# A gated recurrent step on one core: extra products in two places, half-width sampling pieces, one vector instruction moved up

## The reference, cut to what matters

```
def cell(h, x):
    gi = x @ W_ih + b_ih
    gh = h @ W_hh + b_hh
    i_r, i_z, i_n = jnp.split(gi, 3, axis=-1)
    h_r, h_z, h_n = jnp.split(gh, 3, axis=-1)
    r = jax.nn.sigmoid(i_r + h_r)
    z = jax.nn.sigmoid(i_z + h_z)
    n = jnp.tanh(i_n + r * h_n)
    h_new = (1.0 - z) * n + z * h
    return (h_new, h_new)
...
ix = (grid + 1.0) * 0.5 * (L - 1)
x0 = jnp.floor(ix)
w1 = ix - x0
w0 = 1.0 - w1
...
return w0[:, None, :] * v0 + w1[:, None, :] * v1
```

## Time and profile before

| | us |
|---|---|
| median of 3 runs | 2564.22 |
| the profiled execution's own time | 2577.34 |
| span of the profile (first to last instruction) | 2575.6 |
| the loop of 512 steps (first and last r sum A) | 956.6 to 2552.6 |
| PE busy over the span | 2264.0 (88%) |
| DVE, ACT, POOL busy | 1877.2, 1276.6, 526.3 |

### The profile page before, as it was taken

How to read it: one execution, slowest core, us unless ns; L and a number is a source line. 1 busy time by engine, 2 the same in 40 slices (tenths; PEclk the granted TensorE clock), 3 DMA queues, 4 the chain that set the end, 5 groups by cost and what they waited for, 6 DMA issues and landing times. The chain is left out here.

```text
span 2575.6 us, 139739 instructions
## 1 busy us (share of the span) xinstructions
PE 2264.0 (88%) x58516; PEld 1928.8 (75%) x58516; DVE 1877.2 (73%) x8659; ACT 1276.6 (50%) x5568; POOL 526.3 (20%) x2217
## 2 busy tenths in 40 slices
PE   2563689789797889999899999999999999999998
PEld 2552355454454469889899999999999999999996
DVE  5997684683855957887778777777777767777776
ACT  3542484583754744444444544444444444444443
POOL 1002100100101423333322222222222222222221
PEclk9998799899898999999999999999999999999999
DMA  6000000000001000000000000000000000000000
GB/s 230 2 3 1 0 1 1 0 2 1 1 1 49 1 18 5 5 5 5 5 5 5 9 5 9 9 5 9 9 5 9 5 9 9 5 9 9 5 13 20
DMA packets 17205, 32.08 MB, mean 12 GB/s; under 512 B 9664, under 2 KB 9664, under 8 KB 16320
## 3 DMA queue, kind: packets, MB, share of 16 engines
q1 hardware_dynamic: 14320, 22.08, 2.4%
q10 hardware_dynamic: 2256, 1.06, 0.2%
HBM read 18.94 MB, written 4.19 MB: 9 GB/s over the span
## 5 line engine op out<-in xcount | busy, mean ns | idle before, releaser
L1720 PE MATMUL psum<-parts1A,region_w_hh 128*128 128x40 f16 x12288 | 433.1, 179 | 18.7 <-DVE parts1A L1390 12.0
L1720 PE MATMUL psum<-parts0A,region_w_hh 128*128 128x40 f16 x12288 | 434.1, 179 | 16.7 <-DVE parts0A L1390 10.0
L1720 PE MATMUL psum<-parts0B,region_w_hh 128*128 128x40 f16 x12288 | 435.8, 179 | 8.6 <-issue 2.9
L1720 PE MATMUL psum<-parts1B,region_w_hh 128*128 128x40 f16 x12288 | 434.1, 179 | 7.8 <-DVE parts1B L1390 1.9
L1720 PEld LDWEIGHTS psum<-parts1A,region_w_hh 128*128 128x128 f16 x12288 | 373.3, 96 | 29.8 <-DVE parts1A L1390 18.6
L1720 PEld LDWEIGHTS psum<-parts0A,region_w_hh 128*128 128x128 f16 x12288 | 373.2, 96 | 25.7 <-DVE parts0A L1390 14.8
L792 ACT ACTIVATE mixA<-rzA 128x8 f32<-128x8 f32 x512 | 111.0, 217 | 565.5 <-DVE rzA L1342 565.5
L1720 PEld LDWEIGHTS psum<-parts0B,region_w_hh 128*128 128x128 f16 x12288 | 364.4, 96 | 28.6 <-issue 7.5
L1720 PEld LDWEIGHTS psum<-parts1B,region_w_hh 128*128 128x128 f16 x12288 | 362.9, 96 | 26.0 <-DVE parts1B L1390 10.5
L1342 DVE TENSOR_REDUCE rzA<-psum 128x8 f32<-128x32 f32 x512 | 97.6, 191 | 189.3 <-PE psum L1720 179.6
L485 POOL TENSOR_TENSOR addA<-zA,lineA 128x8 f32<-128x8 f32 x512 | 104.5, 204 | 592.5 <-ACT zA L799 592.5
(11 more groups left out here) (257 smaller groups left out, 4047.3 us busy)
## 6 DMA issues: line engine op xcount, KB each, us to landing
region_rows<-in_x_dram SPq DMA_DIRECT2D x4, 1024.0 KB, 12.4
out_dram<-region_w_b SPq DMA_DIRECT2D x16, 256.0 KB, 2.0
region_w_a<-in_L_cond_W_qkv_dram SPq DMA_DIRECT2D x1, 3072.0 KB, 20.0
region_rows<-in_L_cond_W_ih_dram SPq DMA_DIRECT2D x1, 3072.0 KB, 10.8
region_cols<-in_L_cond_W_emb_dram SPq DMA_DIRECT2D x1, 2048.0 KB, 12.8
region_scratch<-in_L_cond_W_hh_dram SPq DMA_DIRECT2D x2, 768.0 KB, 6.2
region_cond<-in_cond_dram ACTq DMA_DIRECT2D x1, 1024.0 KB, 6.4
region_w_out<-in_L_cond_W_out_dram SPq DMA_DIRECT2D x1, 1024.0 KB, 22.1
```

The lines of the kernel that those rows point to most:

```text
L1720: made = e.matmul(k.slots(bank)[:, :, ch, :, 0:2], k.w16[:, part, 2 * read + c, 6 * half + 2 * "rzn".index(g) + ch], k.parts[now][read][:, ...
```

## The change

Three things change, all in the recurrent loop.

1. The extra products stand in two places of a step, after unit ABr and after unit BBn (`SIDE_AFTER`), one contraction chunk in each, where before both chunks stood behind BBn. The same products are made, in the same two steps.
2. The sampling jobs are 160 pieces over 128 steps: each DVE instruction covers 256 columns instead of 512, and five pieces stand in four steps, one in each of three steps and two in the fourth (step 3, 7, 11, ...). Each piece waits for the one before it (`grid`). POOL's two additions keep their 512 and 128 columns; they are queued in the step in which DVE makes the last half of `part`, and wait for it.
3. On DVE keep A stands ahead of r B.

The diff, cut to its core:

```diff
-def sampling_job(j):
-
-    b, r = divmod(j, 24)
-    return (b, r, None) if r < 12 else (b, 12 + (r - 12) % 3, (r - 12) // 3)
+def sampling_job(i):
+
+    j, half = divmod(i, 2)
+    b, r = divmod(j, 20)
+    return (b, r, None, half) if r < 12 else (b, 12 + r % 2, (r - 12) // 2, half)
+
+SAMPLING_JOBS = 160
+
+def sampling_jobs(st):
+
+    return range(min(5 * st // 4, SAMPLING_JOBS), min(5 * (st + 1) // 4, SAMPLING_JOBS))
...
         pool_state(e, k, st, 1)
-        if st < 96:
-            b, r, c = sampling_job(st)
-            if r == 14:
+        for i in sampling_jobs(st):
+            b, r, c, part = sampling_job(i)
+            if r == 13 and part == 1:
                 to = k.sampling[:, b, c]
                 n = 2 * (NC * b + c)
-                e.wait_ge(s["grid"], grid_count(b, 13, c))
+                e.wait_ge(s["grid"], i + 1)
...
-    if r == 14:
-        return
-    if job == 0:
+    cols = slice(half * D // 2, (half + 1) * D // 2)
+    place, fl, integer, left, nxt = (t[:, b, cols] for t in (k.place, k.whole, k.as_int, k.w0, k.right))
+    if i == 0:
         e.wait_ge(s["grid_in"], 16)
     else:
-        e.wait_ge(s["grid"], n - 1)
+        e.wait_ge(s["grid"], i)
...
         dve_n_line(e, k, st, 0)
+        dve_keep(e, k, st, 0)
         dve_r_sum(e, k, st, 1)
-        dve_keep(e, k, st, 0)
         dve_high(e, k, st, 0, nxt)
...
-        if st < 96:
-            dve_sampling_job(e, k, st)
+        for i in sampling_jobs(st):
+            dve_sampling_job(e, k, i)
...
+SIDE_AFTER = ("ABr", "BBn")
...
-        if st in SIDE:
-            (kind, *args), part, parity = SIDE[st]
-            number += part == 0
-            ks = (0, 1) if part == 0 else (2, 3)
...
+            if st in SIDE and u in SIDE_AFTER:
+                (kind, *args), part, parity = SIDE[st]
+                c = 2 * part + SIDE_AFTER.index(u)
+                number += c == 0
```

More of the change, by code:

```diff
@@ L91, in bases_before @@
     return sum(has_base(m) for m in range(n))
-def grid_count(b, r, k):
-    return 20 * b + (r + 1 if r < 12 else 12 + 2 * k + r - 11)
 def side_groups(q):
@@ L1213, in dve_split_inputs, with dve_sampling_job @@
     e.scalar_tensor_tensor(low, source, k.xs[2][:], high, ALU.mult, ALU.subtract).then_inc(s["x_low"], 1)
-def dve_sampling_job(e, k, job):
+def dve_sampling_job(e, k, i):
     s = k.sem
-    b, r, c = sampling_job(job)
-    n = grid_count(b, r, c)
-    place, fl, integer, left, nxt = k.place[:, b], k.whole[:, b], k.as_int[:, b], k.w0[:, b], k.right[:, b]
-    if r == 14:
-        return
-    if job == 0:
+    b, r, c, half = sampling_job(i)
+    cols = slice(half * D // 2, (half + 1) * D // 2)
+    place, fl, integer, left, nxt = (t[:, b, cols] for t in (k.place, k.whole, k.as_int, k.w0, k.right))
+    if i == 0:
         e.wait_ge(s["grid_in"], 16)
     else:
-        e.wait_ge(s["grid"], n - 1)
+        e.wait_ge(s["grid"], i)
     if r == 0:
@@ L1252, in dve_sampling_job @@
         e.wait_ge(s["gates_in_sum"], 12)
-        e.scalar_tensor_tensor(k.sampling[:, b, c], fl, k.feature[:, c:c + 1], left, ALU.is_equal, ALU.mult).then_inc(s["grid"], 1)
+        e.scalar_tensor_tensor(k.sampling[:, b, c, cols], fl, k.feature[:, c:c + 1], left, ALU.is_equal, ALU.mult).then_inc(s["grid"], 1)
     else:
@@ L1257, in dve_sampling_job @@
             e.wait_ge(s["sampling"], 2 * before + 1)
-        e.scalar_tensor_tensor(k.part[:, c % 2], nxt, k.feature[:, c:c + 1], place, ALU.is_equal, ALU.mult).then_inc(s["grid"], 1)
+        e.scalar_tensor_tensor(k.part[:, c % 2, cols], nxt, k.feature[:, c:c + 1], place, ALU.is_equal, ALU.mult).then_inc(s["grid"], 1)
 def dve_add_states(e, k, tile, b, c):
@@ L1724, in pe_gru @@
                 made.then_inc(s[f"{g}_products{h}"], 1)
-        if st in SIDE:
-            (kind, *args), part, parity = SIDE[st]
-            number += part == 0
-            ks = (0, 1) if part == 0 else (2, 3)
[L1729 to L1732, removed]
+            if st in SIDE and u in SIDE_AFTER:
+                (kind, *args), part, parity = SIDE[st]
+                c = 2 * part + SIDE_AFTER.index(u)
+                number += c == 0
+                if kind == "gates":
+                    pe_gate_group(e, k, *args, (c,), SIDE_BANK[parity], number)
+                else:
+                    pe_rows_group(e, k, *args, (c,), SIDE_BANK[parity], number)
 def build(nc, *args):
```

## The result

The changed kernel takes 2597.11 us, the median of 4 runs (2594.74 to 2598.38). The kernel before, run beside it, takes 2562.88 (4 runs, 2561.09 to 2564.81). The ratio is 1.0132, with an interval of 1.0115 to 1.0150: **34.2 us slower**. The forecast was 24.8 us slower, with a range of 2570 to 2604.

The account below looks back on a forecast made before the run. A chain of small instructions through all engines, not PE, was taken to set the step. The terms 2 + 8.7 + 6 + 10.3 + 0.8 - 3 gave +24.8 us on the median 2564.2, so 2589.0 us, range 2570 to 2604.

Parts of the forecast that it names:

- What bounds the kernel: A loop of small instructions through all engines sets the step, 3.01 us; half of the extra products are off it.
- faster by PE: Rival for the whole loop: PE sets the step, so moving extra products gains 43 us, 2529 in all; chance 0.10.
- (a): Extra products in two places, 16-bit steps: a tie, 3.015 instead of 3.01 us, +2 us over 360 steps.
- (b): Extra products in two places, 32-bit steps: half of them takes 0.30 us, +0.09 a step over 96 steps, +8.7 us.
- (c): Gaps among PE's A products, no longer absorbed by the wait for low B: +6 us, bounds 0 and 9.
- (d): POOL's additions start later, waiting for the same step's half piece, and delay its multiplication for A: +10.3 us.
- (e): DVE's half pieces ahead of r sum A: single halves cost nothing, two in a row do; +0.8 us.
- (f): Keep A ahead of r sum B on DVE: high A no longer delayed where r sum B is late, -3 us.
- The lock: Rival: keep A, starting first, blocks POOL's multiplication; high A 0.2 us later in 512 steps, 2690; chance 0.02.
- the argument from keep B: Keep B starts 0.05 us before POOL's multiplication, which runs inside its 0.27 us, so keep A would not block POOL.

Follow-up runs that it names:

- the second profile of before: The kernel before, unchanged, run again for another profile: 2560.29 against 2560.62 us, ratio 1.0001; its profiled execution took 2559.6.
- the shift: Kernel before plus 20 one-column memsets at the start of DVE's program: 2560.57 us, ratio 0.9990; with keep A first as well: 2568.52, ratio 1.0032.
- the spread halves: Kernel before, POOL's additions spread over three steps, DVE's wide pieces halved, never two a step: 2548.57 us; with keep A first as well: 2557.84.
- its two variants: Changed kernel with POOL's additions queued one step later: 2589.38 us, ratio 1.0103; with them spread over three steps: 2579.38 us, ratio 1.0074.
- the first profile of before: The kernel before, unchanged, as profiled for the prediction: that execution took 2577.34 us, against a median of 2564.2.

## Why the prediction was right in sign and short in size

**What bounds the kernel** held. Half of the extra work was off the path, the A start went back to 1.99 as in the earlier trace rows, and the rival "faster by PE" is out: the two places alone cost 8.8 us. POOL's 0.4 behind the B start and high A's 0.33 behind its multiplication came as written.

**(a) and (b), extra products.** Forecast 2 and 8.7. Against the steps without extra products of the same profile (3.013) the changed kernel's steps give 360 x 0.006 = 2.2 and 96 x 0.087 = 8.4; against the second profile of before (3.007) they give 4.3 and 8.9. The choice of 0.30 for half of the 32-bit products was right: the row shows 0.31.

**(c), gaps laid bare.** This is the term that was wrong in sign for the edit alone. The count failed first: I took 86 gaps from one profile as a property of the kernel. A second profile of the same kernel has 44, the kernel with two places 15 and the changed one 37. With 8.8 measured and 11.2 to 11.8 from the steps, (c) was about -3, not +6. That there were fewer gaps fits this; what the lost cover costs by itself was not measured.

**(d), POOL's additions.** Forecast 10.3, measured 11.7 in the 16 steps. POOL began 0.43 (plain), 0.68 (with a split ahead) and 0.93 (two halves) behind the B start; steps became 4.08, 4.34 and 4.6 instead of 3.60, so 0.48, 0.74 and 1.0 more where I had 0.45, 0.71 and 0.97. Of the remainder of 1 us, 0.7 lies in two steps (55 and 90) of 4.43 us, at a granted clock of 1.00, in which high A came 0.68 and not 0.33 behind POOL's multiplication for A, with nothing named that it waited for; the clock, which fell inside two others, took 0.07 in each.

**(e), DVE's pieces.** Forecast +0.8 (its own terms, 4 x 0.28, 4 x 0.55 and 12 x 0.1 less 4.1, give 0.4), measured +5.9 in the other 114 steps. The pieces themselves are as wide as the line through two rows had it (0.484 against 0.48). The largest missing term was not DVE's at all: an idle time of PE of 1.3 us and more, where before the longest in this part was 0.93, and behind it the fall of the clock. In the kernel with the sampling alone the four steps behind a pair of halves with additions (33, 65, 97 and 129) take 3.82 to 3.91, 3.90 in the row shown, where the second profile of before has 3.01 to 3.08. That is 3.4 of the 5 us. In the changed kernel the same four take 3.02 to 3.85. Step 60 is as long, 3.92, but at a granted clock of 1.00: a split and two halves stand ahead of its r sum A, which the forecast had at 0.55, and then DVE comes 0.37 late to low B with nothing named.

**(f), keep A first.** Forecast -3, measured +6.6, and +9.7 and +9.3 in two other pairs. The gain that I forecast is there: over 380 steps the stretch from POOL's multiplication to high A holds 4.6, 5.0 and 3.2 us of lateness with keep A first, 6.2, 7.1 and 5.4 without (the pairs in this order: alone, with the shift, with the spread halves). What outweighs it lies elsewhere: from low B to the B start, where PE is late, it is 15.2, 13.0 and 15.9 us with keep A first and 5.3, 10.6 and 6.7 without, in the same three pairs. The gaps in PE longer than 0.06 us add up to 39.9, 36.2 and 39.9 us against 22.0, 29.3 and 26.4. The kernels with extra products in two places go the same way: counted alike, 11.7 and 16.2 us of gaps with the old order on DVE, and 24.6, 28.3 and 23.6 with keep A first (the changed kernel and its two variants). So the price shows as late instructions on PE. These are single profiles, though, and the first profile of before, 13 us over its median, has 39.8 us of such gaps with keep A in its old place, so they can come for another reason too. That the order on DVE makes them is likely and not shown, and **how the order of two instructions on DVE would bring them about is open**. The shift speaks against the mere place of DVE's instructions, at the one other place that was tried.

**The lock** did not come. POOL's multiplication stayed at 1.11 behind the B start and 0.20 long. But the argument from keep B read only one side of it. Keep A's row, 1380 to 2500 us (count, min/median/max ns), first with keep A first, in the changed kernel, then in the second profile of before:

```profile
L1367 DVE TENSOR_SCALAR keepA<-zA,minus_h_scale x358: 208/276/278, 1382.9 to 2497.0; 128x8 f32<-128x8 f32 x179
```

```profile
L1365 DVE TENSOR_SCALAR keepA<-zA,minus_h_scale x365: 220/233/238, 1380.9 to 2498.2; 128x8 f32<-128x8 f32 x183
```

Keep A takes 0.208 where POOL is away. It starts 0.04 earlier now and is 0.043 longer, so it ends where it ended, 0.03 behind the end of POOL's multiplication. In the step at 1144.42 above it takes 0.66 and ends with POOL's first addition. So keep A ends only when POOL has ended there, and POOL doesn't wait for keep.

Together: extra products 8.8 (forecast 16.7), sampling 17.5 (11.1), keep 6.6 (-3). Two errors of 6 and 10 us to the short side and one of 8 to the long side leave 8 of the 9 us by which the forecast was short. That the result lies inside the range is thus in part luck: (c) and (f) both had the wrong sign, (e) missed its largest term, and the wrong terms partly cancelled. What held on its own is the path, (a), (b) and nearly all of (d).

## What to carry to other kernels

Work that delays another engine must be priced twice: by the wait itself, and by what the long idle time can do to TensorE's clock in the steps behind it (0.8 to 0.9 us in a step here). Waits that the profile names "issue" need a second profile of the same kernel before a term of a sum may rest on them, and a difference of 0.01 us a step is best read against other steps of the same profile. In a chain of small instructions, cut POOL's long instruction into parts that each end before its next due one (11 us here), and keep DVE's instructions with two inputs out of its way.

## What the runs showed of the hardware

- **TensorE's clock.** Idle times of PE of 1.24 to 1.65 us ahead of the A start came with 3.4 us at a granted clock of 0.50, beginning at their end or up to 2.2 us later (7 times after the change, 9 with the sampling alone, 4 and 3 in its two repairs), and one of 1.11 us did too, in the kernel before with POOL's additions spread. Where none was over 0.93 us, in the second profile of before, there was no such stretch. Not every such idle time was followed by one (7 of 13 of 1.3 us or more after the change), and what decides was not tried. The first profile of before has one such stretch too, at the loop's very start (955.8 to 959.2), as has the changed kernel's; they are not in these counts.
- **DVE and POOL in SBUF.** A DVE piece of 0.485 us took 0.95 beside POOL's addition, and up to 1.50; POOL's addition of 1.27 took 1.38. The Trainium skill (SBUF — State Buffer, section Who interferes with whom) says that a DVE instruction with two SBUF inputs contends with a GpSimd instruction that reads SBUF, and by that rule the trace agrees. It also says, of DVE instructions in a two-port mode, that whoever issues first holds the shared ports. Whether keep A runs in such a mode no run shows. Keep A starts 0.05 us ahead of POOL's multiplication and still ends behind it (0.276 long, 0.208 alone): on the starts that the trace records, the measurement does not follow that.
- **PE's gaps come in a grid.** In the traces nearly all gaps stand a multiple of 126 or 127 products apart, and nearly all end 1.2 to 1.6 us after a packet of 16384 bytes has landed on the instruction queue, of which the loop has one every 3.8 us. That PE runs out of instructions at these places fits; that the packets are late because of anything the kernel does was not shown.
